# Two-block recurrent and attention kernel: another order in the first chunk, bank waits split in halves, and the second layer's W2 rounded earlier

## The reference, cut to what matters

```python
def _ffn(x, W1, W2, W3):                 # D = 256, H = 1024
    hidden = jax.nn.silu(x @ W1.T) * (x @ W3.T)
    hidden = fwht(hidden)                # Walsh-Hadamard over the 1024, / sqrt(1024)
    return hidden @ W2.T

for attn in (recurrent, causal_attention):
    xn = layernorm(x)
    s = attn(xn)
    g = silu(_ffn(xn, W1, W2, W3))       # weights of this block
    x = x + s * g
```

## Time and profile before

| what | value |
|---|---|
| median of 3 runs | 355.12 us (355.09 to 355.24) |
| the profiled execution | 355.07 us |
| its span in the trace | 353.3 us |
| TensorE busy | 348.6 us, 99% |
| VectorE busy | 249.8 us, 71% |
| ScalarE busy | 170.5 us, 48% |
| POOL busy | 108.9 us, 31% |
| granted TensorE clock | 1.0 of full speed throughout |

### The profile page before, as it was taken

One profiled execution on the slowest core, in us unless ns is written; L12 is line 12 of the kernel. 1 busy time (PEld: TensorE's weight loads), 2 busy tenths in 40 slices (PEclk: granted clock), 3 DMA queues, 4 the chain that ended last, 5 costly groups with the idle time before them and its releaser, 6 DMA issues.

```text
span 353.3 us, 4946 instructions
## 1 busy us (share of the span) xinstructions
PE 348.6 (99%) x1761; PEld 296.2 (84%) x1761; DVE 249.8 (71%) x491; ACT 170.5 (48%) x336; POOL 108.9 (31%) x125
## 2 busy tenths in 40 slices
PE   8999999999999999999999999999999999999996
PEld 5887888888888888888978878888888888888896
DVE  5679964995499666966588876787657887367624
ACT  2865442447254723454465644654346544464531
POOL 2164410466136933664025030150300703004011
PEclk9999999999999999999999999999999999999999
DMA  7999669206160403140341401436014251064001
GB/s 239 257 184 228 146 112 137 66 33 133 45 138 12 121 0 119 34 119 0 104 146 41 130 2 59 146 76 198 3 52 149 70 158 51 0 193 129 7 0 61
DMA packets 69664, 34.44 MB, mean 97 GB/s; under 512 B 40708, under 2 KB 69640, under 8 KB 69640
## 3 DMA queue, kind: packets, MB, share of 16 engines
q1 hardware_dynamic: 69224, 33.80, 38.3%
q10 hardware_dynamic: 416, 0.33, 0.3%
HBM read 21.99 MB, written 12.12 MB: 97 GB/s over the span
## 4 chain that ended last, share of the span: by engine, by line
PE 96%; ACT 2%; DVE 1%; issue 0%; ACTq 0%
PE GU L360 20%; PE GU L361 20%; PE GU L362 20%; PE O L360 8%; PE O L361 8%; PE O L362 8%; PE GU L527 1%; PE O L428 1%; PE O L509 1%; PE O L510 1%; PE O L508 1%; PE T L362 1%; PE T L361 1%; PE T L360 1%; PE T L367 1%; PE GU L367 1%
## 5 line engine op out<-in xcount | busy, mean ns | idle before, releaser
L724 ACT ACTIVATE hf<-GU 128x512 f32<-128x512 f32 x64 | 38.2, 599 | 79.4 <-DVE hid L851 63.3
L1007 DVE TENSOR_TENSOR hf<-hf,GU 128x512 f32<-128x512 f32 x64 | 43.5, 680 | 28.4 <-PE GU L362 22.6
L360 PE MATMUL GU<-XT,W1T 128*128 128x512 f32 x128 | 50.7, 396 | 0.1
L851 DVE TENSOR_TENSOR hid<-hf,hid 128x512 fp32r<-128x512 f32 x64 | 50.6, 791 | 0.3
L362 PE MATMUL GU<-XT,W1T 128*128 128x512 f32 x128 | 49.9, 390 | 0.0
L361 PE MATMUL GU<-XT,W1T 128*128 128x512 f32 x128 | 49.9, 390 | 0.0
L360 PE MATMUL GU<-XT,W3T 128*128 128x512 f32 x128 | 49.8, 389 | 0.0
L362 PE MATMUL GU<-XT,W3T 128*128 128x512 f32 x128 | 49.8, 389 | 0.0
L361 PE MATMUL GU<-XT,W3T 128*128 128x512 f32 x128 | 49.8, 389 | 0.0
L360 PE MATMUL O<-hid,W2hi 128*128 128x512 f32 x112 | 43.9, 392 | 0.0
L361 PE MATMUL O<-hid,W2hi 128*128 128x512 f32 x112 | 43.7, 390 | 0.0
(11 more groups left out here) (204 smaller groups left out, 727.1 us busy)
## 6 DMA issues: line engine op xcount, KB each, us to landing
swap_rows<-GX SPq DMA_DIRECT2D x7, 512.0 KB, 3.3
sT<-swap_rows SPq DMA_DIRECT2D x28, 128.0 KB, 2.8
swap_gate<-GX SPq DMA_DIRECT2D x7, 512.0 KB, 2.9
sT<-swap_gate SPq DMA_DIRECT2D x28, 128.0 KB, 2.7
stage<-in_L_ffn_W SPq DMA_DIRECT2D x12, 256.0 KB, 4.2
swap_p<-PX SPq DMA_DIRECT2D x4, 640.0 KB, 3.7
PL<-swap_p SPq DMA_DIRECT2D x16, 160.0 KB, 3.1
stage<-in_L_ffn_W SPq DMA_DIRECT2D x32, 64.0 KB, 2.7
```

What stands on the lines that cost most here:

```text
L360: pe.matmul(o, lhs(0), rhs(0), start=start, stop=False)
L724: act.activation(hf[:, c % 2, :], GU[:, c % 2, 0, :], ACT.Silu).then_inc(silu_done, 1)
L851: dve.tensor_tensor(dst, src, hi_part.bitcast(F32), ALU.subtract).then_inc(done, 1)
L1007: dve.tensor_tensor(hf[:, c % 2, :], hf[:, c % 2, :], GU[:, c % 2, 1, :], ALU.mult).then_inc(mul_done, 1)
```

## The change

There are four edits. (1) In the first chunk, the four gate matmuls that need x's high part alone come first, the two with x's low part after them, each k step waiting for its own part. (2) A chunk c >= 2 waits for `silu_done` of chunk c - 2 ahead of its gate half, and for `mul_done` of chunk c - 2 ahead of its up half. (3) For layer 1, `w2_sums` stands behind VectorE's chunk 2 instead of 6, and the two roundings on ScalarE behind chunks 3 and 5 instead of behind all eight. (4) The wait for `sm_lo` 3 moves from the end of TensorE's head to ahead of the Hadamard product behind the up chunks of n = 1, and on VectorE the low part of `hid` 7 of group 0 goes ahead of those of AR and VR.

```diff
--- before.py
+++ after.py
@@ -459,7 +459,7 @@
                 if first and c % 2 == 0:
                     pe.wait_ge(w_lo, c + 2)
                 if c >= 2:
-                    pe.wait_ge(mul_done, 8 * n + c - 1)
+                    pe.wait_ge(silu_done, 8 * n + c - 1)
                 elif first is False and l == 0:
 
                     pe.wait_ge(s_ready, 2 * n) if c == 0 else pe.wait_ge(mul_done, 8 * n)
@@ -467,6 +467,8 @@
 
                     pe.wait_ge(t_ready, 2 * n - 2 * NB + 2) if c == 0 else pe.wait_ge(exp_done, 4 * n - 4 * NB + 4)
                 for g, (w, done) in enumerate(((W1T[l], gate_done), (W3T[l], up_done))):
+                    if c >= 2 and g == 1:
+                        pe.wait_ge(mul_done, 8 * n + c - 1)
                     for k in range(KC):
                         last = mm3(GU[:, c % 2, g, :], lambda a: w[:, a, k, c * P:(c + 1) * P], lambda a: xT[a][k],
                                    k == 0, k == KC - 1)
@@ -474,13 +476,19 @@
 
             def first_up_chunk():
 
-                for g, (w, done) in enumerate(((W1T[0], gate_done), (W3T[0], up_done))):
-                    pe.wait_ge(w_lo, g + 1)
-                    for k in range(KC):
-                        if g == 0:
-                            pe.wait_ge(xt_ready, k + 1)
-                        last = mm3(GU[:, 0, g, :], lambda a: w[:, a, k, 0:P], lambda a: xT[a][k], k == 0, k == KC - 1)
-                    last.then_inc(done, 1)
+                pe.wait_ge(w_lo, 1)
+                for k in range(KC):
+                    pe.wait_ge(xt_hi, k + 1)
+                    for a in (0, 1):
+                        pe.matmul(GU[:, 0, 0, :], W1T[0][:, a, k, 0:P], xT[0][k], start=(k == 0 and a == 0), stop=False)
+                for k in range(KC):
+                    pe.wait_ge(xt_ready, k + 1)
+                    last = pe.matmul(GU[:, 0, 0, :], W1T[0][:, 0, k, 0:P], xT[1][k], start=False, stop=(k == KC - 1))
+                last.then_inc(gate_done, 1)
+                pe.wait_ge(w_lo, 2)
+                for k in range(KC):
+                    last = mm3(GU[:, 0, 1, :], lambda a: W3T[0][:, a, k, 0:P], lambda a: xT[a][k], k == 0, k == KC - 1)
+                last.then_inc(up_done, 1)
 
             def down_chunk(l, n, i):
 
@@ -555,7 +563,6 @@
                 small_av()
                 pe.wait_ge(sm_lo, 1)
                 recurrent_mix(0)
-                pe.wait_ge(sm_lo, 3)
 
             def block0_group(n):
                 if n == 1:
@@ -566,6 +573,8 @@
                     up_chunk(0, n, c, False)
                     if c == 1 and n > 1:
                         next_hadamard(PAIRS + 2 * n - 3)
+                if n == 1:
+                    pe.wait_ge(sm_lo, 3)
                 if n < 3:
                     next_hadamard(PAIRS + 2 * n - 2)
                 recurrent_mix(n)
@@ -684,12 +693,11 @@
                     dst, src = first[q]
                     hi(dst, src, wait, value + q, done)
 
-            def w2_hi(l):
-                half = HC // 2
+            def w2_hi(l, h):
+                part = slice(h * HC // 2, (h + 1) * HC // 2)
                 act.wait_ge(fly_add, l + 1)
                 act.wait_ge(fly, 13 * l + 13)
-                act.activation(W2hi[l][:, 0:half, :], U2[l][:, 0:half, :], ACT.Copy).then_inc(w2hi_ready, 1)
-                act.activation(W2hi[l][:, half:HC, :], U2[l][:, half:HC, :], ACT.Copy).then_inc(w2hi_ready, 1)
+                act.activation(W2hi[l][:, part, :], U2[l][:, part, :], ACT.Copy).then_inc(w2hi_ready, 1)
 
             def first_x_hi():
                 for k in range(KC):
@@ -763,7 +771,8 @@
                 hi(gb[:, :, :].rearrange("p g k -> p (g k)"), O[:, 0, 0:2 * KC], gb_tr, 1, gb_ready)
                 chunk(0, 6, True)
                 hi(flat[0], O[:, 0, :], sm_mm, 1, sm_hi)
-                w2_hi(0)
+                for h in (0, 1):
+                    w2_hi(0, h)
                 chunk(0, 7, True)
                 hid_hi_chunk(0, 7)
                 small_hi([(flat[1], T[:, 0, :]), (flat[2], T[:, 1, :])], 2, sm_mm, 2, sm_hi)
@@ -815,13 +824,13 @@
                     hi(vR[:, 0, 2 * h:2 * h + 2, :].rearrange("p a d -> p (a d)"), O[:, h, :], v_done, 2 * m + h + 1, v_hi)
                 for c in range(HC):
                     chunk(n, c, False)
+                    if prev_layer == 0 and c in (3, 5):
+                        w2_hi(1, c // 4)
                     if c == 4:
                         act.wait_ge(p_moved, 64 * m + 64)
                         for b in range(3):
                             c0, c1 = 4 * b, min(4 * b + 4, BLOCKS)
                             act.activation(blocks_of(0, c0, c1), PL[:, :, c0:c1, :].rearrange("p q c b -> p c q b"), ACT.Copy).then_inc(pt_hi, 1)
-                if prev_layer == 0:
-                    w2_hi(1)
                 hid_hi_chunk(n, HC - 1)
 
             block0_head()
@@ -1115,9 +1124,9 @@
                 w2_lo(0, 1)
                 dve.wait_ge(xrest_loaded, 16)
                 dve.wait_ge(small_loaded, 16 * N_SMALL)
+                hid_lo_chunk(0, HC - 1)
                 small_lo(1)
                 small_lo(2)
-                hid_lo_chunk(0, HC - 1)
 
             def block0_group(n):
                 recurrent_scale(n - 1)
@@ -1164,7 +1173,7 @@
                        vR[:, 0, 2 * h:2 * h + 2, :].rearrange("p a d -> p (a d)"), v_hi, 2 * m + h + 1, v_ready)
                 for c in range(HC):
                     chunk(n, c)
-                    if prev_layer == 0 and c == HC - 2:
+                    if prev_layer == 0 and c == 2:
                         w2_sums(1)
                     between_chunks(n, c, last)
                     if prev_layer == 0 and c == HC - 2:
```

## The result

The changed kernel takes 356.02 us (median of 10 runs, 355.79 to 356.62), the kernel before 355.12 (10 runs, 355.0 to 355.52). The ratio is 1.0025, interval 1.0016 to 1.0033. That is 0.9 us where I forecast 0.5, and 0.12 beyond the upper end of my range.

The account below looks back on a forecast made before the run. TensorE bounds the kernel, with at most about 0.8 us of waits removable. Terms: -0.52 (stall) - 0.25 - 0.03 (down, mix) + 1.17 (POOL delay) + 0.1 = +0.47; span 353.8, forecast 355.6 us, range 354.3 to 355.9.

Parts of the forecast that it names:

- The bound and the unchanged parts: TensorE at full pace but for n=4's waits, at most about 0.8 us to gain; first chunk and bank wait priced 0.
- the 48 waits: Added half waits in the up chunks meet semaphores already passed: priced 0, from above 0.24 us.
- Neither is waited for: the transposes are the cover: First chunk: TensorE's transposes cover x's two low parts, so the new order gains 0, at most 0.16 us.
- The half wait: Up chunk 2 of n=4: gate half waiting for silu alone starts at 180.99 instead of 181.27, gain 0.5 us.
- The turns of VectorE and POOL: n=4: the moved sum and POOL's additions take turns, delaying normalise and the product of chunk 6 by 1.2 us.
- The early W2: Layer 1's W2lo first half and hid 7 come over a microsecond early for the down chunks, gain 0.25 us.
- the last of the sum: Whole execution: span of 353.8 us, from 353.3 before, converted to a forecast time of 355.6 us.
- Same number of instructions, other places: Layer 1's W2 edit: the sum and roundings move without adding instructions.
- (a): Rival: sum finds POOL free or fits VectorE's idle time, delay hidden and gain kept; -0.8, 354.3 us, chance 0.14.
- (b): Rival: delay half hidden, 0.3 to 0.9 left; between -0.5 and +0.2, 354.6 to 355.3 us, chance 0.14.
- (c): Rival: chunk 2's low part loses one more turn, normalise 1.5 us late; +0.8, 355.9 us, chance 0.12.
- (d): Rival: half wait does nothing, chunk 6 stands until chunk 4's product; +1.0, 356.1 us, chance counted with (c).

Follow-up runs that it names:

- e4: Kernel before with only the sm_lo 3 bank wait moved and the low part of hid 7 ahead: 355.26 us against 355.28, ratio 1.0002.
- e1: Kernel before with the half waits alone: 355.27 us against 355.28, ratio 1.0001.
- e8: Changed kernel with layer 1's W2 sum replaced by a same-size transpose reading one SBUF tensor: 354.88 us against 355.26 for the kernel before.
- e2: Kernel before with the W2 edit alone (sum behind chunk 2, roundings behind chunks 3 and 5): 356.31 us against 355.28, ratio 1.003.
- e7: Kernel before with ScalarE's second W2hi rounding in either layer repeating two fulfilled waits, two instructions more: 355.58 us against 355.26, ratio 1.0015.
- e6: As e5, but ScalarE's second rounding does not repeat the first's two waits: 354.49 us against 355.26 for the kernel before, ratio 0.9978.
- e10: Kernel before with ten more instructions on ScalarE, fulfilled waits including e7's two: 355.32 us, ratio 1.0005.
- e11: Kernel before with two more instructions on VectorE, fulfilled waits ahead of the second W2lo of either layer: 355.15 us, ratio 0.9999.
- e5: Changed kernel with layer 1's W2 sum moved behind the low part of hid 7 of n=3: 354.78 us against 355.26 for the kernel before, ratio 0.9987.
- e3: Kernel before with the new gate matmul order in the first chunk alone: 355.21 us against 355.28, ratio 0.9999.
- e9: Kernel before with one more instruction on ScalarE, the two fulfilled waits repeated for layer 0 only: 355.32 us against 355.18, ratio 1.0004.

## Why the prediction was wrong

**The bound and the unchanged parts.** Right for edit 4 (e4) and for the 48 waits (e1, and 21.79 us for n=5's stage). Wrong for edit 1, by little: "Neither is waited for: the transposes are the cover". x's first low part was waited for, and the gain of 0.2 us lies just above the 0.16 that I had put down as the most. In the changed kernel's trace the first gate matmul starts at 9.87, at 9.84 before, which looks like no change only because x's low parts start 0.25 later in that execution, at 9.25.

**The half wait.** Right. The matmuls of chunk 2 start at 181.06, one step of 0.22 after the one before:

```profile
180.84 0.39 PE L362 MATMUL GU<-XT,W3T 128*128 128x512 f32 x1
181.06 0.39 PE L360 MATMUL GU<-XT,W1T 128*128 128x512 f32 x1
```

**The turns of VectorE and POOL.** Right in mechanism and size. Forecast: additions over by 191.3, `normalise` right behind, product of chunk 6 from 197.7 to 198.43, attention product at 198.48, down to 210.38. Measured: 191.33, 197.75, 198.58, 210.44. By the Trainium skill, SBUF — State Buffer, section "Who interferes with whom", a VectorE instruction with one SBUF input outside the two-port modes does not contend with GpSimd, and one with two contends with a GpSimd instruction that reads SBUF. The traces of e8 and the changed kernel agree, 3.29 and 4.42 us for the same additions. What I left open was who would get the first turn. It was VectorE. By my sum it makes no difference for the end, since POOL's last addition sets it; the other order was not seen.

**The early W2.** Right: `hid` 7 is done at 203.12, the third down chunk, which waits for it, starts at 204.99, and the down chunks take 8.20 us.

**A second stall on the way.** Here my sum was a little off. I had the up half of chunk 6 due at 193.2 and the product of chunk 4, which it waits for, at 193.3, and left the tenth out. The weight load there waits 0.32 us, and the matmul behind it is a further tenth late:

```profile
193.36 0.19 PEld L360 LDWEIGHTS GU<-XT,W3T 128*128 128x128 f32 x1 [0.32 <-DVE hf L1016]
```

The last up matmul starts at 197.37, some 0.2 us later than at full pace. It costs nothing, since TensorE would only have stood longer ahead of the attention product: that one is due at 197.60 and starts at 198.58, 0.98 us late where I had about 1.1.

**The step that failed is the last of the sum.** "With the span at 353.8 I forecast 355.6 us": the span came out at 353.8 in the profiled execution and 353.9 in the median of ten, but I carried the 1.8 us around it over from the kernel before, as a term that the change could not touch. They became 2.12 us, and with them the time left the range; with 1.8 it would have been 355.7. The step before it is at fault too: "Same number of instructions, other places". The new `w2_hi` is called once per half and repeats both its waits, so ScalarE's program has two instructions more, seen in the pages as 4948 against 4946 for e2 (4947 for the whole change, since the moved bank wait saves one: e4 has 4945). I had gone through the waits that TensorE gets, and not through those of ScalarE. e7 shows that these two alone, with all work and all stages as before, cost 0.3 us outside the span, and e6 that taking them out gives 0.3 back.

That the span itself was met to a tenth is in part luck. The stage of n=4 grew by 0.46, as worked out; the 0.2 us that the first chunk gained were not in the sum, and tiles that landed later in that execution hid them.

**What stays open.** Why the time around the span hangs on ScalarE's program is not shown. The traces begin with the same instructions at the same times (POOL's first at 0.24 us, SyncE's first DMA issue at 0.74, before, changed and in e7). e10 speaks against a price by the instruction and against a step, since it has e7's two waits and eight more and loses only 0.1 us; e11 speaks against an effect of those two waits on VectorE. Whether the time lies ahead of the span or behind it can't be seen. An effect of the program's place or alignment would not need to grow with the number of instructions, but that is a guess that no run tests.

**The rivals.** (a), delay hidden, fell with the 4.42 us of POOL; its number, -0.8, is what e6 reaches once the sum is elsewhere. (b) and (c) fell too: the delay was 1.21 us and no turn was lost. (d) has no ground: chunk 2 came on time. What it says of chunk 6 is seen in e2, which has no half waits: the attention product starts at 198.96 there, and (d) had 199.0.

## What to carry to other kernels

Before an instruction is moved into an idle hole of one engine, look at what the neighbour does there: a VectorE and a POOL instruction with two SBUF inputs each did not overlap here, and the hole may be a wait for that very neighbour. A hole that ends in a DMA wait with POOL idle (e5) took the same sum at no cost. And a removed stall counts only up to the next wait that was just met: compare starts of the same stage in groups that have the move and groups that have not. An effect that the run-to-run scatter of the time hides can be read from the start of one instruction against its source, as with the first chunk. Last, count the waits that a split function repeats; some become instructions.

## What the runs showed of the hardware that was not expected

The time of an execution outside its trace differs between kernels that do the same work. In the median it was 1.77 to 1.82 us in six kernels (before, e1, e3, e4, e6, e11), 2.10 to 2.15 in five whose ScalarE program has the two repeated waits (the changed kernel, e2, e5, e7, e8), 2.0 in e9 with one of them, and 1.88 in e10, which has both and eight more waits. For changes worth tenths of a microsecond it has to be read from each profiled execution and subtracted.

The landing of the first tiles moves the whole trace from one execution to the next. VectorE's statistics of the second x tile start, before and in e7:

```profile
4.10 0.43 DVE L897 BATCH_NORM_STATS2 bnst<-X 128x6 f32<-128x256 f32 x1 [0.84 <-DMA X<-in_L_attn_x]
```

```profile
4.50 0.43 DVE L899 BATCH_NORM_STATS2 bnst<-X 128x6 f32<-128x256 f32 x1 [0.71 <-DMA X<-in_L_attn_x]
```

e7's stage of n=4 starts at 175.86, that of the kernel before at 175.51. In the changed kernel the same statistics start at 4.40. In e5 it is tiles of weights: the transposes into T wait 0.32 us for their DMA, and the first gate matmul starts at 10.18, at 9.66 in e6, which has the same head. So starts are best compared within a stage, as done here. Spans of the kernel before run from 353.3 to 353.8 us in the 28 executions of the first set.
